# Attention steps of a graph layer without their loop, and half of the gathered rows added on TensorE

## The chip, the cores and the metric

The kernel runs on one core of a Trainium2 chip. The metric is the device time of one execution in microseconds, the median of several runs. The engines are TensorE (PE in the profile; PEld is its weight load), VectorE (DVE), ScalarE (ACT), GpSimd (POOL) and SyncE (SP, which only issues transfers here).

## The reference

One layer over 2500 nodes with 256 features and 80000 edges: a graph attention, a mixing product and a mixture of eight experts. The change touches the attention alone. What it computes, cut to the part that matters:

```python
xl = (x @ W_l).reshape(N, HEADS, HEAD_DIM)      # 4 heads of 64
xr = (x @ W_r).reshape(N, HEADS, HEAD_DIM)
e = xl[src] + xr[dst]
e = jnp.where(e >= 0, e, NEG_SLOPE * e)
score = jnp.einsum('ehd,hd->eh', e, att)
m = jax.ops.segment_max(score, dst, num_segments=N)
ex = jnp.exp(score - m[dst])
denom = jax.ops.segment_sum(ex, dst, num_segments=N)
alpha = ex / (denom[dst] + SM_EPS)
agg = jax.ops.segment_sum(alpha[:, :, None] * xl[src], dst, num_segments=N)
```

The edges are sorted by `dst`.

## The kernel before

The attention stage, `attend`, goes through the sorted edges in 176 steps, called quads, of four groups (G = 4) of 128 edges. Eight quads are a run (RUN), two runs a turn (RING = 16 quads), and there are 11 turns. `over_quads` writes out the first and the last turn and puts the nine between into a loop, so an engine holds 16 quads of code for them; addresses and semaphore thresholds in the loop come from registers. Every engine runs its own version of the same loop over quads, and semaphores tie them together. For quad q:

- SyncE loads `e_drow` (the target of each edge, spread over 128 partitions, L964) and `e_xr` (128 rows of xr, each split in three bf16 parts, L965) into four rotating buffers, and stores the running sums of the quad 16 steps back (L980).
- GpSimd gathers the four groups of xl rows, 128 x 260 fp32 each, with one indirect transfer per group (L1014). There are buffers for 16 quads, and the gather of quad q waits for the product of quad q - 16 (`prod`). The indices of a run of eight quads are first copied from `src_cols` to `e_idx` (L1007), twice per turn.
- VectorE makes the selection matrix `e_sel` two quads ahead (L1031). TensorE multiplies it with `e_xr` (`edges`, L1218: 4 groups x 3 parts, 12 bf16 products of 256 columns), which gives xr[dst] of every edge in two PSUM banks; banks alternate by quad.
- VectorE adds the gathered rows to these (`sum_edges`, L1040, two operations of 128 x 512), takes the positive part times the attention weights over all four groups (`relus`, L1048, 128 x 1024) and sums it by head (`scores`, L1055). The linear part of the leaky relu comes with the gathered row.
- Eleven quads later ScalarE takes the exponent (L1297) and multiplies the gathered rows with it, 16 copies of 128 x 64 (L1301, `e_prod`). Twelve quads later TensorE sums these by target with a selection matrix that VectorE makes (L1063): `sums`, L1262, four fp32 products of 260 columns, each of which the trace shows as two passes. VectorE adds the result to the running sums (`add_sums`, L1077).
- At the end of each run, in the first five quads of the next, the maxima of the run's scores are found: scans on VectorE, transposes on TensorE, a decay on ScalarE. I call these the closing steps. ScalarE's products of a run wait for its `e_diff` (L1147).

The order on an engine is that in which its `quad` function calls these parts. Engines execute in order, so an instruction that waits holds up all that stands behind it on its engine. Where the text below says step, a quad is meant.

## Time and profile before

| | us |
|---|---|
| median of three runs | 1959.8 (1956.9 to 1965.11) |
| profiled execution | 1963.8 |
| its span | 1962.1 |
| busy: TensorE, VectorE | 1224.7, 1141.8 |
| busy: ScalarE, GpSimd | 870.3, 796.9 |
| first gather starts | 229.1 |
| last gather starts | 1468.7 |

The span is what the engines' records cover; the profiled execution's own time has 1.7 us around it. The attention stage lies between about 229 and 1542 us. Busy times say what an engine executed, not what set the end; the timelines of several engines over the same few microseconds say who stood still while who worked. "Idle before" in brackets is the time an engine stood before a row, with what released it: an instruction of another engine, "issue" (nothing that the profile shows) or "remote" (a semaphore whose setter isn't seen).

### The profile page before, as it was taken

How to read it: one execution, taken by the hardware profiler on the slowest of the kernel's cores; microseconds unless marked ns; L12 is line 12 of the kernel's file. 1: busy time of each engine (PE TensorE's matmuls, PEld its weight loads, DVE VectorE, ACT ScalarE, POOL GpSimd, SP SyncE). 2: the span in 40 equal slices, each digit the busy share in tenths (PEclk: the TensorE clock that was granted, in tenths of full speed). 3: DMA queues.
4: the chain of work that ended last, by engine and by line, in shares of the span. 5: the costliest groups of instructions: out<-in, count | busy, mean ns of one | idle time of the engine just before them, and what ended most of it. 6: DMA issues, size and time to landing. Idle time of an engine off the chain costs nothing. (4 is left out here: it accounts for less than half of the span.)

```text
span 1962.1 us, 24702 instructions
## 1 busy us (share of the span) xinstructions
PE 1224.7 (62%) x5321; PEld 869.1 (44%) x5321; DVE 1141.8 (58%) x2208; ACT 870.3 (44%) x3346; POOL 796.9 (41%) x907
## 2 busy tenths in 40 slices
PE   2599513666666666566666765655657696499950
PEld 1476302444444444444544554444445465255530
DVE  3670215787777776787878776767766382000018
ACT  0241000556565655666665665656649422122211
POOL 3111372455555555555555555554540412200014
PEclk9998755788787887888898777877868865699985
DMA  4220243465555655565656555555540500144403
GB/s 155 78 93 13 70 117 90 122 155 140 146 135 154 158 145 142 142 159 138 165 149 163 147 155 141 146 144 135 152 119 31 154 1 21 49 119 119 118 27 95
DMA packets 161282, 230.60 MB, mean 118 GB/s; under 512 B 36421, under 2 KB 134078, under 8 KB 160766
## 3 DMA queue, kind: packets, MB, share of 16 engines
q1 hardware_dynamic: 121220, 124.33, 21.8%
q0 software_dynamic: 37056, 102.46, 21.0%
q10 hardware_dynamic: 2880, 2.66, 0.4%
q14 instruction: 110, 0.89, 0.2%
q8 instruction: 16, 0.26, 0.1%
HBM read 186.36 MB, written 42.99 MB: 117 GB/s over the span
## 5 line engine op out<-in xcount | busy, mean ns | idle before, releaser
L1014 POOL DMA_INDIRECT e_xl<-d_xl,e_idx x704 | 670.6, 953 | 544.0 <-ACT e_prod L1301 310.4
L1301 ACT ACTIVATE e_prod<-e_xl,e_prod 128x64 f32<-128x64 f32 x2816 | 692.3, 334 | 10.9 <-issue 5.0
L1262 PE MATMUL bank<-e_prod,e_selt 128*128 128x260 f32 x1408 | 460.9, 484 | 210.2 <-ACT e_prod L1301 133.7
L1262 PEld LDWEIGHTS bank<-e_prod,e_selt 128*128 128x128 f32 x1408 | 322.2, 240 | 303.2 <-issue 223.4
L1218 PE MATMUL bank<-e_xr,e_sel 128*128 128x256 bf16 x2112 | 327.1, 309 | 160.0 <-issue 112.9
L1218 PEld LDWEIGHTS bank<-e_xr,e_sel 128*128 128x128 bf16 x2112 | 232.2, 111 | 245.6 <-issue 172.0
L1040 DVE TENSOR_TENSOR e_edge<-bank,e_xl 128x512 f32<-128x512 f32 x352 | 224.9, 678 | 165.4 <-remote 118.9
L1048 DVE SCALAR_TENSOR_TENSOR e_edge<-e_edge,bank 128x1024 f32<-128x1024 f32 x176 | 212.6, 1208 | 0.1
L1055 DVE TENSOR_REDUCE e_score<-e_edge 128x16 f32<-128x1024 f32 x176 | 212.3, 1206 | 0.3
L1297 ACT ACTIVATE e_prod<-e_diff 128x16 f32<-128x16 f32 x176 | 39.1, 222 | 304.8 <-remote 196.6
L1077 DVE SCALAR_TENSOR_TENSOR e_acc<-e_acc,keep_cols,bank 128x260 f32<-128x260 f32 x154 | 72.9, 473 | 133.6 <-remote 77.9
L1710 DVE COPY f_y<-bank 98x256 f32<-98x256 f32 (+1 forms) x32 | 11.3, 417 | 227.3 <-PE bank L1681 227.3
L1063 DVE TENSOR_TENSOR e_selt<-bank,cyclic_cols 128x512 f32<-128x512 f32 x176 | 119.7, 680 | 0.0
L1290 ACT ACTIVATE e_rr<-e_drop 1x4 f32<-1x4 f32 x22 | 4.5, 205 | 251.0 <-DVE e_drop L1128 153.2
L1667 PE MATMUL bank<-f_rowst,w_rows 128*128 128x391 f32 x256 | 88.7, 505 | 5.5 <-ACT f_rowst L1691 4.9
L1743 POOL MEMSET c_subst<- 128x512 f32 x3 | 1.4, 523 | 220.2 <-POOLq L1626 220.2
L1673 PE MATMUL bank<-f_hid,w_rows 128*128 128x391 f32 x256 | 85.5, 491 | 0.0
L1031 DVE TENSOR_SCALAR e_sel<-e_drow,lane 128x512 bf16<-128x512 bf16 x176 | 63.1, 359 | 10.0 <-DMA e_xr<-d_xr 9.9
L1667 PEld LDWEIGHTS bank<-f_rowst,w_rows 128*128 128x128 f32 x256 | 49.0, 194 | 41.8 <-issue 9.3
L1673 PEld LDWEIGHTS bank<-f_hid,w_rows 128*128 128x128 f32 x256 | 48.4, 189 | 35.8
L1695 ACT ACTIVATE f_hid<-bank,b_cols 128x391 f32<-128x391 f32 x64 | 37.6, 588 | 57.1 <-PE bank L1667 57.1
L1246 PE MATMUL bank<-ident,e_tops 128*128 128x128 f32 x22 | 8.8, 402 | 74.0 <-DVE e_tops L1141 74.0
(310 smaller groups left out, 1131.4 us busy)
## 6 DMA issues: line engine op xcount, KB each, us to landing
e_xr<-d_xr SPq DMA_DIRECT2D x176, 192.0 KB
d_hist<-e_acc SPq DMA_DIRECT2D x176, 130.0 KB
e_drow<-d_rel SPq DMA_DIRECT2D x176, 128.0 KB
w_rows<-in_L_ffn_w_dram SPq DMA_DIRECT2D x16, 1024.0 KB
e_xl<-d_xl,e_idx POOLq DMA_INDIRECT x704
e_rows<-d_rows SPq DMA_DIRECT2D x22, 192.5 KB
d_xr<-a_xr SPq DMA_DIRECT2D x20, 192.0 KB
d_in<-zero SPq DMA_DIRECT2D x3, 1024.0 KB
```

The source lines that it names most:

```text
L1014: pool.indirect_dma_start(xl[:, q.slot * G + g, :], None, m.d_xl, bass.IndirectOffsetOnAxis(ap=idx[p][:, at:at + 1], axis=0)).then_inc(gat ...
L1031: dve.tensor_scalar(sel[:, b, :], drow[:, r, :], m.lane[:, 0:1], None, ALU.is_equal).then_inc(s["sel"], 1)
L1040: dve.tensor_tensor(edge[:, b, 2 * i:2 * i + 2, :], ps_edge[b][i][:, :].rearrange("p (g c) -> p g c", g=2), xl[:, q.slot * G + 2 * i:q.slo ...
L1048: dve.scalar_tensor_tensor(out=edge[:, b, :, :], in0=edge[:, b, :, :], scalar=0.0, in1=att_relu.unsqueeze(1).to_broadcast([P, G, DIM]), op ...
L1055: dve.tensor_reduce(score[:, p, :, q.at * G:q.at * G + G].rearrange("p h g -> p g h"), edge[:, b, :, :].rearrange("p g (h c) -> p g h c", ...
L1063: dve.tensor_tensor(selt[:, b, :, :], lane_up.unsqueeze(1).to_broadcast([P, G, P]), m.cyclic[:, bass.ds(q.k * G, G)].unsqueeze(2).to_broad ...
L1077: dve.scalar_tensor_tensor(out=flat(acc[:, r, :, :]), in0=flat(before), scalar=m.keep[:, bass.ds(q.k, 1)], in1=ps_agg[q.slot % 2], op0=ALU ...
L1218: last = pe.matmul(ps_edge[b][g // 2][:, g % 2 * DIM:g % 2 * DIM + DIM], sel[:, b, g * P:g * P + P], xr[:, r, part * DIM:part * DIM + DIM] ...
L1262: last = pe.matmul(ps_agg[b], selt[:, b, g, :], flat(prod[:, b, g, :, :]), start=(g == 0), stop=(g == G - 1))
L1301: last = act.activation(prod[:, b, g, h, 0:HEAD], xl[:, q.slot * G + g, h * HEAD:h * HEAD + HEAD], ACT.Copy, scale=prod[:, b, g, h, HEAD:H ...
L1667: last = pe.matmul(m.bank[2 + f % 2][:, 0:CAP], w1[:, q, half, f * P:f * P + P], rowst[:, half, :], start=(half == 0), stop=(half == 1))
L1673: last = pe.matmul(m.bank[4 + out][:, 0:CAP], w2[:, q, f, out * P:out * P + P], hid[:, f, :], start=(f == 0), stop=(f == FCH - 1))
```

## The change

- The loop is gone: all 176 quads are written out on each engine, with constant addresses and thresholds.
- GpSimd's copy of indices is gone. The gathers take their indices from `src_cols`.
- TensorE adds the gathered rows of groups 0 and 1 itself: after the three bf16 parts of a group follows one fp32 product of the gathered rows with an identity matrix into the same sums. It takes groups 2 and 3 first, then waits for the gathers of its quad, then groups 0 and 1. The identity (128 x 128) is the weight, the 256 columns of gathered rows move past it.
- VectorE adds only groups 2 and 3. The relu of groups 0 and 1 reads PSUM directly, with the attention weights from SBUF; groups 2 and 3 have a relu of their own.
- TensorE's products of quad q now wait for the relu of quad q - 2 on groups 0 and 1, which frees the bank, and for the sum on 2 and 3.

```diff
-def over_quads(eng, body, behind=0):
-    for slot in range(RING):
-        body(Quad(0, slot))
-    with eng.Fori(1, TURNS - 1) as turn:
-        for slot in range(RING):
-            body(Quad(turn, slot))
-    for slot in range(RING + behind):
-        body(Quad(TURNS - 1, slot))
+def over_quads(body, behind=0):
+    for k in range(QUADS + behind):
+        body(Quad(k // RING, k % RING))
...
             def quad(q):
-                p = q.slot // RUN
-                if q.at == 0:
-                    if q.since(2 * RUN):
-                        pool.wait_ge(s["summed"], 2 * q.k - 2 * RUN)
-                    pool.tensor_copy(idx[p][:, :], m.idx[:, bass.ds(q.run * SUBS_RUN, SUBS_RUN)]).then_inc(s["idx"], 1)
-                    pool.wait_ge(s["idx"], q.run + 1)
                 if q.since(RING):
                     pool.wait_ge(s["prod"], q.k - RING + 1)
                 settle(pool, m)
                 for g in range(G):
-                    at = q.at * G + g
+                    at = q.k * G + g
                     pool.indirect_dma_start(xl[:, q.slot * G + g, :], None, m.d_xl, bass.IndirectOffsetOnAxis(
-                        ap=idx[p][:, at:at + 1], axis=0)).then_inc(gathered[q.slot], 16)
+                        ap=m.idx[:, at:at + 1], axis=0)).then_inc(gathered[q.slot], 16)
...
-                for i in range(2):
-                    dve.tensor_tensor(edge[:, b, 2 * i:2 * i + 2, :],
-                                      ps_edge[b][i][:, :].rearrange("p (g c) -> p g c", g=2),
-                                      xl[:, q.slot * G + 2 * i:q.slot * G + 2 * i + 2, 0:DIM], ALU.add).then_inc(s["summed"], 1)
+                dve.tensor_tensor(edge[:, b, 2:4, :], ps_edge[b][1][:, :].rearrange("p (g c) -> p g c", g=2),
+                                  xl[:, q.slot * G + 2:q.slot * G + 4, 0:DIM], ALU.add).then_inc(s["summed"], 1)
...
-                dve.wait_ge(s["summed"], 2 * q.k + 2)
-                dve.scalar_tensor_tensor(out=edge[:, b, :, :], in0=edge[:, b, :, :], scalar=0.0,
-                                         in1=att_relu.unsqueeze(1).to_broadcast([P, G, DIM]),
+                dve.scalar_tensor_tensor(out=edge[:, b, 0:2, :], in0=ps_edge[b][0][:, :].rearrange("p (g c) -> p g c", g=2), scalar=0.0,
+                                         in1=m.att_relu[:, :].unsqueeze(1).to_broadcast([P, 2, DIM]),
+                                         op0=ALU.max, op1=ALU.mult).then_inc(s["relu"], 1)
+                dve.wait_ge(s["summed"], q.k + 1)
+                dve.scalar_tensor_tensor(out=edge[:, b, 2:4, :], in0=edge[:, b, 2:4, :], scalar=0.0,
+                                         in1=att_relu.unsqueeze(1).to_broadcast([P, 2, DIM]),
                                          op0=ALU.max, op1=ALU.mult).then_inc(s["relu"], 1)
...
                 if q.since(2):
-                    pe.wait_ge(s["summed"], 2 * q.k - 2)
-                for g in range(G):
+                    pe.wait_ge(s["summed"], q.k - 1)
+                    pe.wait_ge(s["relu"], 2 * q.k - 3)
+                for g in (2, 3, 0, 1):
+                    out = ps_edge[b][g // 2][:, g % 2 * DIM:g % 2 * DIM + DIM]
                     for part in range(3):
-                        last = pe.matmul(ps_edge[b][g // 2][:, g % 2 * DIM:g % 2 * DIM + DIM], sel[:, b, g * P:g * P + P],
-                                         xr[:, r, part * DIM:part * DIM + DIM], start=(part == 0), stop=(part == 2))
+                        last = pe.matmul(out, sel[:, b, g * P:g * P + P], xr[:, r, part * DIM:part * DIM + DIM],
+                                         start=(part == 0), stop=(part == 2 and g >= 2))
+                    if g < 2:
+                        if g == 0:
+                            pe.wait_ge(gathered[q.slot], (q.turn + 1) * 64)
+                        last = pe.matmul(out, m.ident[:, :], xl[:, q.slot * G + g, 0:DIM], start=False, stop=True)
                 last.then_inc(s["edges"], 1)
```

What this makes of the order on three engines. First VectorE, one plain quad inside the loop before; ISA and REGISTER_ALU are register work:

```order
L1040 TENSOR_TENSOR e_edge<-bank,e_xl 128x512 x2
L1031 TENSOR_SCALAR e_sel<-e_drow,lane 128x512
L1047 ISA
L1048 SCALAR_TENSOR_TENSOR e_edge<-e_edge,bank 128x1024
L1077 REGISTER_ALU
L1077 SCALAR_TENSOR_TENSOR e_acc<-e_acc,keep_cols,bank 128x260
L1063 ISA
L1063 TENSOR_TENSOR e_selt<-bank,cyclic_cols 128x512
L1055 TENSOR_REDUCE e_score<-e_edge 128x4x4
```

and the same quad after (line numbers are those of the changed kernel):

```order
L1026 TENSOR_TENSOR e_edge<-bank,e_xl 128x512
L1018 TENSOR_SCALAR e_sel<-e_drow,lane 128x512
L1032 SCALAR_TENSOR_TENSOR e_edge<-bank,att_relu 128x512
L1036 SCALAR_TENSOR_TENSOR e_edge<-e_edge,bank 128x512
L1065 SCALAR_TENSOR_TENSOR e_acc<-e_acc,keep_cols,bank 128x260
L1051 TENSOR_TENSOR e_selt<-bank,cyclic_cols 128x512
L1043 TENSOR_REDUCE e_score<-e_edge 128x4x4
```

One of two sums has gone, the relu is in two halves of which the first no longer follows a sum, and the register work is gone. Then TensorE, the products of two quads with the sums between them, inside the loop before:

```order
L1213 REGISTER_ALU
L1215 ISA
L1218 MATMUL bank<-e_xr,e_sel 128x256 x12
L1257 REGISTER_ALU
L1262 MATMUL bank<-e_prod,e_selt 128x260 x4
L1213 REGISTER_ALU
L1215 ISA
L1218 MATMUL bank<-e_xr,e_sel 128x256 x12
```

and after:

```order
L1208 MATMUL bank<-e_xr,e_sel 128x256 x9
L1213 MATMUL bank<-e_xl,ident 128x256
L1208 MATMUL bank<-e_xr,e_sel 128x256 x3
L1213 MATMUL bank<-e_xl,ident 128x256
L1256 MATMUL bank<-e_prod,e_selt 128x260 x4
```

Two fp32 products stand in the quad's products, the first behind nine bf16 ones, and the sums come after them. Last GpSimd, the start of a run inside the loop before:

```order
L1007 ISA
L1007 COPY e_idx<-src_cols 128x32
L1008 REGISTER_ALU
L1010 REGISTER_ALU
L1014 DMA e_xl<-d_xl,e_idx 128x260 x4
```

and the whole stage after, from its last memset on:

```order
L993 MEMSET e_acc 128x1040
L1001 DMA e_xl<-d_xl,src_cols 128x260 x704
L947 UNCONDITIONAL_BRANCH
```

Nothing but waits stands between the gathers any more.

## Rows read from the trace of the kernel before

**Rows 1.** The page's busy table: us, share of the span, instructions.

```profile
PE 1224.7 (62%) x5321; PEld 869.1 (44%) x5321; DVE 1141.8 (58%) x2208; ACT 870.3 (44%) x3346; POOL 796.9 (41%) x907
```

**Rows 2.** The page's groups: count | busy, mean ns | idle before.

```profile
L1014 POOL DMA_INDIRECT e_xl<-d_xl,e_idx x704 | 670.6, 953 | 544.0 <-ACT e_prod L1301 310.4
...
L1218 PE MATMUL bank<-e_xr,e_sel 128*128 128x256 bf16 x2112 | 327.1, 309 | 160.0 <-issue 112.9
...
L1040 DVE TENSOR_TENSOR e_edge<-bank,e_xl 128x512 f32<-128x512 f32 x352 | 224.9, 678 | 165.4 <-remote 118.9
L1048 DVE SCALAR_TENSOR_TENSOR e_edge<-e_edge,bank 128x1024 f32<-128x1024 f32 x176 | 212.6, 1208 | 0.1
```

**Rows 3.** Stretches of line L1055 alone, both halves of one turn: start:end, length.

```profile
837.50:891.20 53.70, 9.63 (x8) 0.85 0.59 153
891.20:945.40 54.20, 9.65 (x8) 0.81 0.58 148
```

**Rows 4.** One turn: PE, PEld, DVE, ACT, POOL busy, PEclk, DMA share, GB/s.

```profile
504.00:617.00 113.00, 73.30 (x336) 52.99 (x336) 84.72 (x148) 66.80 (x278) 59.87 (x65) 0.77 0.54 141
```

**Rows 5.** Waits between 504 and 1391 us: total, times, longest.

```profile
POOL e_xl L1014 <- ACT e_prod L1301: 228.2, 58, 7.7
...
DVE e_acc L1077 <- remote: 84.7, 16, 8.2
...
DVE e_edge L1040 <- remote: 68.6, 30, 6.4
```

**Rows 6.** VectorE's timeline, 641 to 656 us: start, us, operation [idle before].

```profile
641.18 1.28 DVE L1040 TENSOR_TENSOR e_edge<-bank,e_xl 128x512 f32<-128x512 f32 x2
642.38 0.56 DVE L1031 TENSOR_SCALAR e_sel<-e_drow,lane 128x512 bf16<-128x512 bf16 x1
642.86 1.20 DVE L1048 SCALAR_TENSOR_TENSOR e_edge<-e_edge,bank 128x1024 f32<-128x1024 f32 x1
643.98 0.47 DVE L1077 SCALAR_TENSOR_TENSOR e_acc<-e_acc,keep_cols,bank 128x260 f32<-128x260 f32 x1
...
652.62 1.29 DVE L1040 TENSOR_TENSOR e_edge<-bank,e_xl 128x512 f32<-128x512 f32 x2 [6.43 <-remote]
```

**Rows 7.** GpSimd's timeline around 520 us and around 650 us.

```profile
520.87 0.22 POOL L1007 COPY e_idx<-src_cols 128x32 int32 x1
521.98 0.97 POOL L1014 DMA_INDIRECT e_xl<-d_xl,e_idx  x1 [0.89 <-POOL e_idx L1007]
...
648.14 0.95 POOL L1014 DMA_INDIRECT e_xl<-d_xl,e_idx  x1 [0.30 <-issue]
649.39 0.95 POOL L1014 DMA_INDIRECT e_xl<-d_xl,e_idx  x1 [0.30 <-issue]
```

**Rows 8.** ScalarE's timeline from 536 us and from 646 us on.

```profile
536.02 3.93 ACT L1301 ACTIVATE e_prod<-e_xl,e_prod 128x64 f32<-128x64 f32 x16
...
646.88 0.35 ACT L1301 ACTIVATE e_prod<-e_xl,e_prod 128x64 f32<-128x64 f32 x1 [0.37 <-issue]
648.27 0.35 ACT L1301 ACTIVATE e_prod<-e_xl,e_prod 128x64 f32<-128x64 f32 x1 [1.04 <-issue]
```

**Rows 9.** TensorE's timeline from 536 us on, at half, then at full clock.

```profile
536.01 3.81 PE L1262 MATMUL bank<-e_prod,e_selt 128*128 128x260 f32 x8 [4.01 <-ACT e_prod L1301]
539.61 2.44 PE L1218 MATMUL bank<-e_xr,e_sel 128*128 128x256 bf16 x12
541.89 1.92 PE L1262 MATMUL bank<-e_prod,e_selt 128*128 128x260 f32 x8
543.64 1.47 PE L1218 MATMUL bank<-e_xr,e_sel 128*128 128x256 bf16 x12
```

**Rows 10.** The first gathers: VectorE's longest idle, and GpSimd after its copy.

```profile
276.33 1.29 DVE L1040 TENSOR_TENSOR e_edge<-bank,e_xl 128x512 f32<-128x512 f32 x2 [26.00 <-remote]
...
270.18 0.97 POOL L1014 DMA_INDIRECT e_xl<-d_xl,e_idx  x1 [0.81 <-POOL e_idx L1007]
```

More of the change, by code:

```diff
@@ L887, in exists @@
         return not self.known() or 0 <= self.k < QUADS
-def over_quads(eng, body, behind=0):
-    for slot in range(RING):
-        body(Quad(0, slot))
-    with eng.Fori(1, TURNS - 1) as turn:
-        for slot in range(RING):
-            body(Quad(turn, slot))
-    for slot in range(RING + behind):
-        body(Quad(TURNS - 1, slot))
+def over_quads(body, behind=0):
+    for k in range(QUADS + behind):
+        body(Quad(k // RING, k % RING))
 def attend(nc, ctx, m, a):
     sb = lambda name, shape, dt=F32: ctx.enter_context(nc.sbuf_tensor(name, shape, dt))
-    s = sem_set(nc, m.sems, "att", "init idx sel edges summed relu score lin turned run top ends heads fwd bwd carried drop cols raised tops topped diff rr f fac ex prod selt agg old acc rows* links fixed")
+    s = sem_set(nc, m.sems, "att", "init sel edges summed relu score lin turned run top ends heads fwd bwd carried drop cols raised tops topped diff rr f fac ex prod selt agg old acc rows* links fixed")
     loaded = [m.sems.enter_context(nc.semaphore(f"att_loaded{r}")) for r in range(4)]
@@ L908, in attend @@
     gathered = [m.sems.enter_context(nc.semaphore(f"att_gathered{r}")) for r in range(RING)]
-    idx = [sb(f"e_idx{q}", [P, SUBS_RUN], I32) for q in range(2)]
     xl = sb("e_xl", [P, RING * G, ROW])
@@ L989, in _ @@
             sp.wait_ge(s["init"], 1)
-            over_quads(sp, quad, behind=STORE_LAG)
+            over_quads(quad, behind=STORE_LAG)
             for r in range(4):
@@ L1012, in quad @@
                 for g in range(G):
-                    at = q.at * G + g
+                    at = q.k * G + g
                     pool.indirect_dma_start(xl[:, q.slot * G + g, :], None, m.d_xl, bass.IndirectOffsetOnAxis(
-                        ap=idx[p][:, at:at + 1], axis=0)).then_inc(gathered[q.slot], 16)
-            over_quads(pool, quad)
+                        ap=m.idx[:, at:at + 1], axis=0)).then_inc(gathered[q.slot], 16)
+            over_quads(quad)
         @block.vector
@@ L1053, in scores @@
                 b, p = q.slot % 2, q.slot // RUN
-                dve.wait_ge(s["relu"], q.k + 1)
+                dve.wait_ge(s["relu"], 2 * q.k + 2)
                 dve.tensor_reduce(score[:, p, :, q.at * G:q.at * G + G].rearrange("p h g -> p g h"),
@@ L1205, in _ @@
                 select(Quad(0, k))
-            over_quads(dve, quad, behind=CLOSE_LAG)
+            over_quads(quad, behind=CLOSE_LAG)
         @block.tensor
@@ L1281, in quad @@
                     carry_cols(o)
-            over_quads(pe, quad, behind=CLOSE_LAG)
+            over_quads(quad, behind=CLOSE_LAG)
         @block.scalar
@@ L1322, in _ @@
             act.wait_ge(s["init"], 4)
-            over_quads(act, quad, behind=WEIGH_LAG)
+            over_quads(quad, behind=WEIGH_LAG)
 def node_update(nc, ctx, m, a):
```

## The prediction

> **What bounds the kernel now.** I read the busy table first. No engine is full: TensorE has 62% of the span, VectorE 58% [rows 1]. The costly groups all lie in the attention stage, and the longest in wall time is GpSimd's: 704 gathers of 953 ns, four to a step of 128 x 4 edges [rows 2]. On GpSimd's timeline inside a burst one gather follows the other every 1.25 us (0.95 busy, 0.30 issue), so the four of a step take 5.0 us [rows 7]. The stage's 176 steps therefore cannot take less than 176 x 5.0 = 880 us.
>
> The table by stretches says how long a step does take: 54 us for 8 steps in either half of a 16-step turn, 6.75 each [rows 3], and 113 us for 16 steps in another turn [rows 4], 7.1 each. I use 6.9. VectorE alone would do it in 4.7: on its timeline two sums take 1.20 from start to start of the next operation, and the whole step runs without a gap [rows 6]. Gathers alone would do it in 5.0. What is added is the interplay of the two, and the timelines of one stretch on four engines show it.
>
> Between 645 and 652.6 us GpSimd issues gathers without a break [rows 7], VectorE stands still for 6.43 us, released by "remote" [rows 6], and ScalarE, whose sixteen copies depend on nothing but each other, executes single ones 0.35 us long with 0.37 or 1.04 us between their end and the next start instead of back to back [rows 8]. So this is no missing operand: while a burst of gathers lasts, the other engines crawl. I call it a hold. It ends when GpSimd has run out of gathers it may issue, here 2.3 us after the last one (650.34 to 652.62). The first steps show it naked: GpSimd issues 64 gathers in a row there, and VectorE has one idle of 26.00 us [rows 10]. In the stretch 504 to 1391 the holds cost VectorE 84.7 + 68.6 = 153 us, and GpSimd in turn waits 228.2 us for ScalarE's products (which free the buffers of the step 16 back) [rows 5]. The kernel swings between the two: burst, hold, buffers run out, the others work, the next burst. That swing sets the end; the busy times matter only by what they do to it.
>
> **The change part by part.** The sum is made against the profiled execution, 1963.8 us (span 1962.1); the median of the three runs is 4.0 lower.
>
> *Index copies.* Once per run of 8 steps GpSimd copied 32 columns of indices: 0.22 for the copy and 0.89 until the next gather, against 0.30 between others [rows 7], so 0.81 too much. 22 times: 17.8 us. GpSimd is always inside a burst there, so I take it whole: -18. Bounds 0 and -24 (22 x 1.11).
>
> *VectorE.* Per step two sums and one 1024-wide product go; one sum and two 512-wide products come. From start to start: before 1.20 + 1.12 = 2.32 (641.18 to 642.38, and 642.86 to 643.98) [rows 6]; a 512-wide operation takes 0.60 of that, so three take 1.80. A 512-wide relu that reads PSUM isn't in the trace; it is nearest to the sum, which also reads PSUM (678 ns) [rows 2]. Saved 0.52 per step, 92 us of work over 176. Where does it reach the end? Not in a hold, and not where GpSimd is late anyway. It does in the three closing steps of each of 22 runs, where GpSimd waits for ScalarE, ScalarE for VectorE: 66 x 0.52 = 34, of which I take half, 17, because some of these steps lie beside bursts. And in some 17 steps at the start (after the first 64 gathers) and after the last gather: 9. Together -26; bounds 0 and -92.
>
> *TensorE.* Two fp32 products per step come, each two passes, 704 passes in all. A pass of 260 columns is 1.92 / 8 = 0.24 us long at full clock and 3.81 / 8 = 0.48 at half [rows 9]; both clocks occur all the time, since the granted clock is 0.77 of full over a turn [rows 4], near the middle of 1.2 and 2.4 GHz. So a step gets 0.96 or 1.9 us more on TensorE, 169 to 335 us in all. Cover: TensorE is idle for about 40 of 113 us in a turn [rows 4], and the projection products of a step are ready before VectorE asks for them. The cover fails in one place: after a long hold TensorE starts at half clock, does sums (3.81), then the products of the next step (2.44) [rows 9], and these are used at once. There the added 1.9 minus the about 1.0 that VectorE also comes earlier (two steps of 0.52) is exposed: 0.9, at the 16 long waits of "DVE e_acc <- remote" [rows 5]: +14. Bounds 0 and +335. TensorE now also waits for the gathers of its step, with the sums of the step 12 back queued behind; a gather is issued when the product of the step 16 back is done and products lag 11 steps, so about 5 steps ahead, 5 x 6.9 = 34 us, and I cost this at nothing. If that lead were gone, each step would wait for a gather, up to 5 us.
>
> *The loop.* Register arithmetic for addresses and thresholds goes from every engine: by the order of instructions some 17 per step, against 8 more for TensorE and 1 or 2 for VectorE. On a free engine these are hidden behind data work (VectorE's step has no gap [rows 6]). In a hold every instruction is slow, so fewer of them ought to help: about 7 fewer of about 108 per step. 7% of the 153 us of holds [rows 5], carried from 128 to 144 steps: -12. Bounds 0 and -170 (all holds gone). The loop's backward branch costs nothing that I can see: the half turn that holds it takes 54.2 us, the other 53.7 [rows 3].
>
> The Trainium skill (Runtime: NRT & Kernel Launch, "Instruction fetch mechanics") says that a taken branch to a target outside two pages of instructions stalls until a DMA has fetched it, and that written-out code avoids this. By that rule the unrolling would be the larger part of the gain; rows 3 show no such cost, and the sum above leaves it out.
>
> Sum: 1963.8 - 18 - 26 + 14 - 12 = 1921.8; less the 4.0 between profiled run and median: 1918.
>
> **The rivals.** *TensorE becomes the bound (slower), 0.27.* The granted clock of 0.77 means that nearly half the time is at half clock. If that share of the 144 middle steps, 144 x 0.46 = 66, pays 1.9 and saves only 0.52, it is 66 x 1.38 = +91; with the copies' -18 and the 4.0 it is 2033. If half of it is covered, 1987. It decides from the point at which TensorE ends a step's products later than VectorE ends the relu of the step before. For it: TensorE at half clock needs 3.81 + 2.44 + 1.9 = 8.2 us for a step, more than the 6.9 of today. Against it: at full clock 1.92 + 1.47 + 0.96 = 4.4 [rows 9], and TensorE works off its queue during holds.
>
> *Nothing moves, 0.14.* If a cycle is only gathers (5.0 per step) and ScalarE's first product after a hold, neither VectorE's nor TensorE's work counts, and some of the copies' time is given back: 1963.8 - 9 - 4 = 1951 to 1965. For it: ScalarE needs 3.93 us for the sixteen copies of a step whatever VectorE does [rows 8], and GpSimd's waits are waits for ScalarE [rows 5].
>
> *The back edge does cost, 0.10.* A hold lies at the end of each turn. If its 4.5 us were the branch (10 turns), 45 us would go beside the rest: 1918 - 45 = 1873. Against it: an equal hold stands in mid turn and the halves are equal [rows 3].
>
> *Longer holds, 0.07.* The 26.00 us hold ended at 276.33, 6 us after GpSimd's copy had left its gap at 270.18 [rows 10]. If these gaps let the others through and are gone, each of 22 runs may lose some 3 us: +66 - 40 = 1990.
>
> The forecast keeps 0.42.
>
> **How the numbers follow.** A measurement of this kernel can tell about 0.5%, 10 us, from no change, so "faster" is under 1950 and "slower" over 1970. Faster: 0.42 + 0.10 and a little of the second rival, 0.55. Same: 0.14. Slower: 0.31. The forecast's own range, with VectorE's and the holds' terms at a third or double, is 1885 to 1950. The stated range reaches to the branch rival and to the half-covered TensorE rival: 1862 to 2000. The likeliest time is 1918.
>
> **What would show it.** In the changed profile GpSimd must show 704 gathers at the same 1.25 us with no copy between. VectorE's step should be near 4.2 where nothing holds it. If the forecast is right, the steps per turn of 16 (where the loop had its turns) take 102 to 108 us, and the "remote" waits of VectorE stay, a little shorter. If TensorE has become the bound, VectorE's sum waits for TensorE's new fp32 line rather than for "remote", and the time is over 1980. If the holds are gone or halved, instruction count or branch was their cause and my time is far too high. The prediction fails, too, if the added instructions of TensorE count as much for the holds as the removed register work.

## The result: slower by 1.4%, or faster by 4%, by whether the chip held its engines

In the comparison for which the forecast was made the kernel before took 1961.0 us (median) and the changed kernel 1982.7: ratio 1.0143, interval 1.0072 to 1.0213. Forecast were 1918 and "faster". The time is inside the stated range (1862 to 2000), outside the forecast's own (1885 to 1950), and the direction is wrong. Ratios and their 95% intervals compare fast runs only, while the times beside them are medians of all runs, so a few pairs of times don't divide to their ratio.

One fact has to come first. The changed kernel was compared three times, each time beside the kernel before on one chip, and came out on both sides:

| comparison | before, us | changed, us | ratio (interval) | holds in the traces |
|---|---|---|---|---|
| first | 1961.0 | 1982.7 | 1.014 (1.007 to 1.021) | yes |
| `after_again` | 1659.3 | 1597.0 | 0.960 (0.954 to 0.966) | none in steady work |
| `after_third` | 1937.7 | 1992.0 | 1.029 (1.020 to 1.039) | yes |

The holds, on which the whole prediction was built, are not a property of the kernel alone. Of seven comparisons five had them and two did not. The kernel before tells the two apart by its time, 1938 to 1961 us or 1659 to 1663, and within a comparison all kernels are alike, save those to which a long pause was added. The results number the chips, and two numbers (4 and 7) occur once in either condition.

**The profile after (first comparison).** The page's busy table, against [rows 1]:

```profile
PE 1336.2 (68%) x6025; PEld 946.2 (48%) x6025; DVE 1047.5 (53%) x2208; ACT 869.9 (44%) x3346; POOL 789.4 (40%) x885
```

VectorE has 94 us less work, TensorE 112 us more. The page's groups (count | busy, mean ns | idle before), against [rows 2]:

```profile
L1001 POOL DMA_INDIRECT e_xl<-d_xl,src_cols x704 | 668.7, 950 | 599.3 <-ACT e_prod L1295 368.2
...
L1213 PE MATMUL bank<-e_xl,ident 128*128 128x256 f32 x704 | 243.9, 432 | 12.4 <-issue 6.8
L1026 DVE TENSOR_TENSOR e_edge<-bank,e_xl 128x512 f32<-128x512 f32 x176 | 119.6, 680 | 244.1 <-remote 197.8
...
L1032 DVE SCALAR_TENSOR_TENSOR e_edge<-bank,att_relu 128x512 f32<-128x512 f32 x176 | 119.2, 677 | 0.0
L1036 DVE SCALAR_TENSOR_TENSOR e_edge<-e_edge,bank 128x512 f32<-128x512 f32 x176 | 118.3, 672 | 0.0
```

Each operation costs what it was expected to: the relu that reads PSUM 677 ns, as the sum. But the idle before VectorE's sum rose from 165.4 to 244.1 us, and GpSimd's idle from 544.0 to 599.3. The stretch of [rows 5], in the columns of [rows 4]; in each pair the first line is of the scores' line alone (L1043, L1055), so its count is the number of steps. After:

```profile
504.00:1391.00 887.00, 149.33 (x124) 0.84 0.56 143
...
504.00:1391.00 887.00, 634.55 (x3109) 461.51 (x3110) 588.56 (x1140) 518.16 (x2155) 471.00 (x496) 0.84 0.56 143
```

Before:

```profile
504.00:1391.00 887.00, 154.29 (x128) 0.81 0.57 148
...
504.00:1391.00 887.00, 562.43 (x2688) 413.54 (x2688) 674.76 (x1169) 532.59 (x2213) 490.93 (x528) 0.81 0.57 148
```

VectorE's work per step went from 674.76 / 128 = 5.27 to 588.56 / 124 = 4.75, that is 0.52 less, as the prediction said. The step went from 887 / 128 = 6.93 to 887 / 124 = 7.15. The waits of the same stretch say what took its place, against [rows 5]:

```profile
POOL e_xl L1001 <- ACT e_prod L1295: 251.3, 57, 12.4
...
DVE e_edge L1026 <- remote: 111.6, 27, 11.2
...
DVE e_acc L1065 <- remote: 96.2, 17, 9.2
...
DVE e_run L1081 <- DMA x_rows<-in_x_dram: 42.5, 7, 9.2
```

VectorE's two "remote" waits were 153 us and are 208, and a third line (L1081, put down to a DMA that was issued in the first 10 us of the kernel and can't be what it waits for) stands in holds for another 42.5. In the kernel before that line (L1093) had 6.1. One of these holds, on GpSimd's, then VectorE's timeline (start, us, operation [idle before]); eleven more gathers follow the first without a wait:

```profile
486.05 0.94 POOL L1001 DMA_INDIRECT e_xl<-d_xl,src_cols  x1 [7.94 <-ACT e_prod L1295]
...
499.80 0.95 POOL L1001 DMA_INDIRECT e_xl<-d_xl,src_cols  x1 [0.30 <-issue]
508.28 0.94 POOL L1001 DMA_INDIRECT e_xl<-d_xl,src_cols  x1 [7.53 <-ACT e_prod L1295]
...
494.72 0.68 DVE L1036 SCALAR_TENSOR_TENSOR e_edge<-e_edge,bank 128x512 f32<-128x512 f32 x1
503.40 0.42 DVE L1081 TENSOR_TENSOR_SCAN e_run<-e_rows,bank 128x128 f32<-128x128 f32 x1 [8.01 <-DMA x_rows<-in_x_dram]
```

If a pause of over 1.5 us ends a burst, bursts of twelve gathers or more were 18 of 70 between 400 and 1350 us in the trace before, and are 28 of 64 now. In the rows above a burst runs, VectorE is held for 8 us, GpSimd then waits 7.5 us for ScalarE, and the next burst starts.

The first steps have the longest holds. GpSimd issues its first 64 gathers from 230.56 us on without a gap, and VectorE stands twice:

```profile
262.98 0.69 DVE L1026 TENSOR_TENSOR e_edge<-bank,e_xl 128x512 f32<-128x512 f32 x1 [16.28 <-remote]
...
307.78 0.69 DVE L1026 TENSOR_TENSOR e_edge<-bank,e_xl 128x512 f32<-128x512 f32 x1 [41.40 <-remote]
```

So a hold can end for one step in the middle of a burst, at 262.98 here, with no copy near it.

TensorE's new line shows 1.06 us for the two passes of a product at half clock and 0.60 at full. From its start to the start of the next product it is 0.85 and 0.44, where the prediction had 0.96 and 0.48:

```profile
505.57 2.12 PE L1208 MATMUL bank<-e_xr,e_sel 128*128 128x256 bf16 x9
507.49 1.06 PE L1213 MATMUL bank<-e_xl,ident 128*128 128x256 f32 x2
508.34 0.84 PE L1208 MATMUL bank<-e_xr,e_sel 128*128 128x256 bf16 x3
...
512.74 0.60 PE L1213 MATMUL bank<-e_xl,ident 128*128 128x256 f32 x2
513.18 0.49 PE L1208 MATMUL bank<-e_xr,e_sel 128*128 128x256 bf16 x3
```

### The profile page after: what moved, and what is told of

Same layout as the page of the kernel before. It is cut to its first block and busy times, and to the rows that moved or that the text cites. A ratio compares the mean times of both kernels' runs of the same rounds, so it can differ in the third digit from the quotient of the medians.

```text
span 1978.6 us, 23673 instructions
## 1 busy us (share of the span) xinstructions
PE 1336.2 (68%) x6025; PEld 946.2 (48%) x6025; DVE 1047.5 (53%) x2208; ACT 869.9 (44%) x3346; POOL 789.4 (40%) x885
## 5 line engine op out<-in xcount | busy, mean ns | idle before, releaser
L1001 POOL DMA_INDIRECT e_xl<-d_xl,src_cols x704 | 668.7, 950 | 599.3 <-ACT e_prod L1295 368.2
L1256 PE MATMUL bank<-e_prod,e_selt 128*128 128x260 f32 x1408 | 405.0, 431 | 125.2 <-ACT e_prod L1295 48.8
L1208 PE MATMUL bank<-e_xr,e_sel 128*128 128x256 bf16 x2112 | 351.0, 305 | 171.1 <-issue 86.8
L1256 PEld LDWEIGHTS bank<-e_prod,e_selt 128*128 128x128 f32 x1408 | 285.7, 212 | 215.6 <-issue 153.9
L1208 PEld LDWEIGHTS bank<-e_xr,e_sel 128*128 128x128 bf16 x2112 | 225.7, 108 | 286.7 <-issue 204.5
L1213 PE MATMUL bank<-e_xl,ident 128*128 128x256 f32 x704 | 243.9, 432 | 12.4 <-issue 6.8
L1026 DVE TENSOR_TENSOR e_edge<-bank,e_xl 128x512 f32<-128x512 f32 x176 | 119.6, 680 | 244.1 <-remote 197.8
L1043 DVE TENSOR_REDUCE e_score<-e_edge 128x16 f32<-128x1024 f32 x176 | 212.1, 1205 | 0.3
L1213 PEld LDWEIGHTS bank<-e_xl,ident 128*128 128x128 f32 x704 | 126.1, 223 | 22.1 <-issue 7.7
L1032 DVE SCALAR_TENSOR_TENSOR e_edge<-bank,att_relu 128x512 f32<-128x512 f32 x176 | 119.2, 677 | 0.0
L1036 DVE SCALAR_TENSOR_TENSOR e_edge<-e_edge,bank 128x512 f32<-128x512 f32 x176 | 118.3, 672 | 0.0
```

What stands on the lines that cost most here:

```text
L1001: pool.indirect_dma_start(xl[:, q.slot * G + g, :], None, m.d_xl, bass.IndirectOffsetOnAxis(ap=m.idx[:, at:at + 1], axis=0)).then_inc(gath ...
L1026: dve.tensor_tensor(edge[:, b, 2:4, :], ps_edge[b][1][:, :].rearrange("p (g c) -> p g c", g=2), xl[:, q.slot * G + 2:q.slot * G + 4, 0:DIM ...
L1032: dve.scalar_tensor_tensor(out=edge[:, b, 0:2, :], in0=ps_edge[b][0][:, :].rearrange("p (g c) -> p g c", g=2), scalar=0.0, in1=m.att_relu[ ...
L1036: dve.scalar_tensor_tensor(out=edge[:, b, 2:4, :], in0=edge[:, b, 2:4, :], scalar=0.0, in1=att_relu.unsqueeze(1).to_broadcast([P, 2, DIM]) ...
L1043: dve.tensor_reduce(score[:, p, :, q.at * G:q.at * G + G].rearrange("p h g -> p g h"), edge[:, b, :, :].rearrange("p g (h c) -> p g h c", ...
L1208: last = pe.matmul(out, sel[:, b, g * P:g * P + P], xr[:, r, part * DIM:part * DIM + DIM], start=(part == 0), stop=(part == 2 and g >= 2))
```

## The experiments

**Theories.** H: where holds occur, they give back what is saved. P: TensorE's added passes are the cost. U: the written-out code, or the missing index copies, are. C (added after the first four experiments): the sign hangs on whether holds occur.

### Both halves of the change alone

`e_unroll_only` has the changed kernel's loops and the additions of before:

```
-                dve.tensor_tensor(edge[:, b, 2:4, :], ps_edge[b][1][:, :]...
+                for i in range(2):
+                    dve.tensor_tensor(edge[:, b, 2 * i:2 * i + 2, :], ...
```

> The 176 steps written out and the index copies gone, but all four groups added on VectorE as before: half of the change. Theory H (holds give back what is saved: every engine but GpSimd crawls while gathers run without a break, and anything that lets GpSimd issue longer bursts lengthens them): the loss comes from denser bursts, some of it from the copies' gaps gone; 1950 to 1975 us. Theory P (the loss is TensorE's added fp32 passes): without them the prediction's own terms for copies and instructions hold, 1961 - 18 - 12 = 1931. Theory U (written-out code is itself the loss): as slow as the changed kernel, 1983 or more.

`e_pe_add_only` has the loop and the index copies, with the changed kernel's sum_edges, relus and edges:

> The loop and the index copies stay; groups 0 and 1 are added in PSUM by the fp32 identity product: the other half of the change. Theory H: VectorE's saved 0.52 us a step is given back by longer holds, and TensorE's new work is not itself late; 1955 to 1980. Theory P: the fp32 passes cost 14 to 91 us in the prediction's working and VectorE's saving gives 26 at most; 1980 to 2000, with VectorE waiting for TensorE's fp32 line. Theory U: 1961 - 26 + 14 = 1949 or less.

`e_no_add` is the changed kernel less its identity products, so it leaves out the gathered rows of groups 0 and 1:

```
-                    if g < 2:
-                        if g == 0:
-                            pe.wait_ge(gathered[q.slot], (q.turn + 1) * 64)
-                        last = pe.matmul(out, m.ident[:, :], xl[:, q.slot * G + g, 0:DIM], start=False, stop=True)
```

> The changed kernel without the two identity products of a step: groups 0 and 1 are left without their gathered rows (that addition is left out), so VectorE has its saving of 0.52 us a step and TensorE no more work than before. Theory H: still no gain to speak of, 1950 to 1980, with holds as long as in the changed kernel. Theory P: the prediction's sum without TensorE's term, 1918 - 14 = 1904, up to 1930. Theory U: between, 1983 - 14 = 1969.

`e_copies` is the changed kernel with this back in front of each 8 steps' gathers:

```
+                    pool.tensor_copy(idx[p][:, :], m.idx[:, bass.ds(q.run * SUBS_RUN, SUBS_RUN)]).then_inc(s["idx"], 1)
+                    pool.wait_ge(s["idx"], q.run + 1)
```

> The changed kernel with GpSimd's index copy of 32 columns put back once per 8 steps. Theory H, gap form (the copies' gaps shortened holds): faster than the changed kernel by 5 to 20 us, 1963 to 1978. Theory H, plain form (a gap of 0.8 us once in 32 gathers is too rare to matter): 1980 to 1990. The prediction's term for the copies: 18 us slower than the changed kernel, 2001.

Measured, in one comparison in which the kernel before took 1663.4 us: 1623.7 (ratio 0.975, 0.971 to 0.980), 1611.9 (0.969, 0.963 to 0.974), 1584.6 (0.954, 0.950 to 0.959) and 1617.0 (0.972, 0.968 to 0.976). No theory had such times, since there were no holds: no engine has a wait for "remote", and GpSimd issued its 704 gathers with no gap over 0.9 us in three of the four (1.8 in e_unroll_only). They are the change's parts without holds, to be read with the next comparison. Of the four only two were repeated where holds occur; the copies put back and the loop with the identity products were not, so there the copies and the loop are not told apart.

### The two kernels themselves, without holds

`after_again` and `before_again` are unchanged.

> The changed kernel itself. In the four runs before this, GpSimd issued its 704 gathers without a single wait and no engine was held; the kernel before took 1663 us there and 1961 where the first comparison was made. Theory C (the sign hangs on the chip: where holds occur they give everything back, where they don't the gathers' 5.1 us per step or VectorE's step is the bound): without holds the changed kernel takes 1605 to 1620 against 1663, ratio 0.965 to 0.975; with holds 1.01 to 1.02 at 1960 to 2000. Theory P (TensorE's work costs 14 to 91 us everywhere): ratio over 1.0 in either case.

> The kernel before, for its profile on the chip of this comparison. Theory C: without holds VectorE is busy over 95% of the attention stage, since its step of about 5.3 us (closing work in it) is longer than the four gathers of 5.0, and GpSimd issues without waits; 1663 us. With holds: as in the first profile, VectorE 76% busy, 1961 us.

Measured: 1597.0 against 1659.3, and 1666.7 for the profiled kernel before. Theory C has the sign, though the ratio of 0.960 lies a little under its 0.965 to 0.975; theory P falls in its strict form. What bounds each is plain in these traces. Before, 400 to 1000 us, the scores' line alone and then all engines (VectorE is the third pair); the groups of the page's kind below:

```profile
400.00:1000.00 600.00, 130.39 (x109) 0.87 0.72 187
...
400.00:1000.00 600.00, 432.18 (x2264) 326.33 (x2262) 569.20 (x997) 449.23 (x1882) 423.13 (x457) 0.87 0.72 187
...
L1040 DVE TENSOR_TENSOR e_edge<-bank,e_xl 128x512 f32<-128x512 f32 x352 | 224.1, 675 | 11.2 <-DMA e_xl<-d_xl,e_idx 9.1 <-issue 1.9
```

600 / 109 = 5.5 us a step (5.3 expected), VectorE busy 95%, and 11.2 us of idle before its sum where [rows 2] have 165.4. The changed kernel:

```profile
400.00:1000.00 600.00, 142.49 (x119) 0.97 0.78 203
...
L1001 POOL DMA_INDIRECT e_xl<-d_xl,src_cols x704 | 671.3, 954 | 214.4 <-issue 200.7 <-ACT e_prod L1295 13.7
```

600 / 119 = 5.04 us, four gathers at 1.25; of 214.4 us between gathers 200.7 are issue. It is bound by GpSimd's gathers.

In this condition the parts can be priced. VectorE's saving, within one comparison: 1623.7 - 1584.6 = 39 us; the prediction had 26. The index copies: e_copies less the changed kernel is 0.972 - 0.960 = 0.012 of 1660, 19 us; the prediction had 18. TensorE's products: 0.960 - 0.954 = 0.006, 10 us; it had 14. The last two are differences between two comparisons and are known to 12 us either way, so TensorE's is not clear of zero. And the loop's back edge, which it had at nothing: ScalarE's timeline of before_again where a turn begins,

```profile
399.75 0.30 ACT L1310 COPY e_fwd_link<-links 1x128 bf16 x1 [2.07 <-issue]
...
403.18 0.23 ACT L1297 ACTIVATE e_prod<-e_diff 128x16 f32<-128x16 f32 x1 [2.94 <-issue]
```

5.0 us in which ScalarE waits for nothing that the profile shows. The same pair stands at the start of each of the eight turns behind a branch, 4.4 to 6.7 us together, and in e_unroll_only nowhere. VectorE pays 3.45 us a step later, behind TensorE's transposes. VectorE's line L1103, the copy that waits there, in before_again, and the same line (L1090) in e_unroll_only:

```profile
  PE bank L1235: 29.7, 9
...
  PE bank L1222: 0.5, 1
```

29 us go with the loop. The first step of a turn took 9.0 to 10.4 us in before_again in each of the eight turns behind a branch, and 6.3 where none lay before it and in every turn of e_unroll_only. The Trainium skill's rule (Runtime: NRT & Kernel Launch, "Instruction fetch mechanics": a taken branch out of the fetched pages stalls for its target) agrees with this, 1.7 to 3.9 us at a time on ScalarE; the trace shows the idle time, not the fetch. In [rows 3] it didn't show beside the holds.

### The same parts where holds occur

> The changed kernel without the identity products (groups 0 and 1 are left without their gathered rows, as in the earlier run of it), on another chip. Where holds occur, theory H expects no gain over the kernel before, 1950 to 1980 us, since VectorE's saving alone lengthens the bursts; theory P (TensorE's work is what costs there) expects 1880 to 1930. Where none occur it repeats 0.954 of the kernel before within 0.005, 10 us under the changed kernel.

> The steps written out and the index copies gone, all additions on VectorE as before, once more. Where holds occur, the changed kernel without its identity products came out at 0.998 of the kernel before. Theory H (any work saved comes back as holds) expects about the same here, 0.99 to 1.01. If written-out code alone lengthens the bursts and VectorE's saving does help, this is slower than that, 1.01 to 1.03; if VectorE's saving is what feeds the bursts, faster, 0.97 to 0.985. Without holds it repeats 0.975.

Measured: the changed kernel without its identity products 1953.9 us against 1955.5 (0.998, 0.993 to 1.003); the written-out kernel with all additions on VectorE 1954.4 against 1943.8 (1.005, 1.001 to 1.009). With the changed kernel's 1.014 and 1.029 beside them: writing out, worth 40 us without holds, is worth nothing; VectorE's 0.5 us a step is worth 0.7% (14 us, between 1 and 26); TensorE's products cost 1.7 to 3.2%, 32 to 61 us, not 10. These are differences between comparisons too, known to 12 to 21 us, but both of TensorE's are clear of zero. The next experiment, which does have the products, lies 32 us over e_no_add_2 in the same comparison. The trace of e_no_add_2 shows how the saving goes (scores' line; all engines; waits of 504 to 1391 us):

```profile
504.00:1391.00 887.00, 153.42 (x127) 0.81 0.56 147
...
504.00:1391.00 887.00, 556.50 (x2670) 407.83 (x2668) 600.93 (x1155) 530.99 (x2209) 484.77 (x511) 0.81 0.56 147
...
DVE e_acc L1065 <- remote: 123.4, 20, 8.6
DVE e_run L1081 <- DMA x_rows<-in_x_dram: 51.2, 8, 8.0
DVE e_edge L1026 <- remote: 41.2, 22, 7.0
```

VectorE works 600.93 / 127 = 4.73 a step instead of 5.27, and the step is still 6.98. Its three kinds of hold are 216 us, and the same three lines of the kernel before 84.7 + 68.6 + 6.1 = 159. Whatever the line and the releaser, VectorE's idle times of over 2 us in this stretch are 232 us (42 of them) instead of 164 (30): 68 us more, and 127 x 0.54 = 69 us was saved. So VectorE's saving comes back as holds, as theory H has it. For TensorE's part theory P has the size right, but not the way: VectorE hardly waits for TensorE's new line, 23.7 us before its sum in the changed kernel against 24.8 for the projection products in this one. The cost, too, appears as "remote".

### GpSimd's lead

> The changed kernel, but GpSimd may gather a step's rows only when the product of the step 14 back is done, not 16 back: it can be 3 steps ahead of VectorE instead of 5. Where holds occur, theory H (a hold lasts until GpSimd has used up the gathers it may issue) expects each hold 5 to 8 us shorter, and 1850 to 1960 us against the changed kernel's 1983; a hold that ends by itself after a time would stay, and the shorter lead then costs: 1990 to 2050. Where none occur (1597 before) GpSimd is the bound and has had no credit to spare: 1597 to 1615, with waits of GpSimd for ScalarE's products of a few us.

```
-                    pool.wait_ge(s["prod"], q.k - RING + 1)
+                    pool.wait_ge(s["prod"], q.k - 13)
```

Measured: 1985.7 against 1955.5 (1.018, 1.008 to 1.028), as the changed kernel. The expectation was wrong on both counts: the time lies in neither range. Bursts of twelve are 27, as 28 in the changed kernel, and VectorE's two "remote" waits 205 us, as 208. So what ends a burst is not the lead alone. My reading, not shown by a run, is that ScalarE's products made while the burst runs feed it, and two steps less of lead shift VectorE against GpSimd and leave the cycle as it is.

### A pause between the gathers

The changed kernel with a memset behind the gathers of a step; only its width, or how often it comes, differs:

```
+                if q.k:
+                    pool.wait_ge(s["pause"], q.k)
+                pool.memset(pause[:, :], 0.0).then_inc(s["pause"], 1)
```

> The changed kernel with a memset of 128x1280 on GpSimd behind the four gathers of every step, about 1.2 us each with nothing else added: a step's gathers take 6.3 us instead of 5.1. Where holds occur, theory H (a hold needs a long unbroken burst) expects most of them gone and 1800 to 1930 us; if a hold needs only the number of gathers, not their density, the time stays at 1980 or rises to 2100. Where none occur, theory C (gathers alone are the bound of the changed kernel there) expects 176 x 1.2 = 211 us more than the changed kernel, about 1820; if VectorE or TensorE were the bound, less than half of it.

> The changed kernel with the memset of 128x1280 on GpSimd behind the four gathers of each step, once more, in the hope of a chip on which holds occur. There, theory H in its density form (a hold needs about 6 us of gathers without a break, and 1 us of pause every 5 us lets the other engines through) expects holds rarer and 1780 to 1930 us; if a hold follows from a number of gathers and not from their density, 1985 to 2100. Without holds it repeats 1.064 of the kernel before, 6.06 us a step.

> The changed kernel with a memset of 128x16 on GpSimd behind the four gathers of each step: hardly any time, about 0.1 us, but an instruction of another kind between them. Where holds occur: if it is the other instruction that lets the engines through, holds go and it takes 1600 to 1640 us; if it is the idle microsecond of the gather queue, they stay and it takes 1960 to 2000. Without holds: 1597 to 1620.

> The same with 128x512, which adds some 0.4 us to a step's 5.0: 5.4 us. Density theory: somewhere between no pause (holds in most steps) and 1 us (none) is the point; here, if below it, 1640 to 1680 us with and without holds; if above it, holds remain, 1850 to 1980 where they occur, and 1640 to 1680 elsewhere.

> The memset of 128x1280, but only behind every second step: 1.06 us after 8 gathers in a row, 10.0 us, so on average the same pause as the half one. Where holds occur, they begin 5 to 7 us after a burst does, so the theory of the unbroken burst expects them to stay (1850 to 1980), and the theory of the mean rate expects the same time as the half pause. Without holds: 1670 to 1700.

> The changed kernel with a memset of 128x1024 on GpSimd behind the four gathers of each step, about 0.8 us net: 5.8 us a step. A pause of 0.37 us left all holds, 1.06 us left none. If the point lies under 0.8, 1720 to 1750 us with and without holds elsewhere, and that is then the fastest version that no session slows; if it lies over it, 1850 to 1970 where holds occur.

| kernel | memset | added per step, us | us | kernel before, us | ratio (interval) |
|---|---|---|---|---|---|
| e_pause_min | 128x16 | 0.0 | 2004.9 | 1953.0 | 1.031 (1.022 to 1.041) |
| e_pause_half | 128x512 | 0.4 | 1966.3 | 1953.0 | 1.009 (1.004 to 1.013) |
| e_pause_second | 128x1280, every second step | 0.5 | 1968.8 | 1953.0 | 1.012 (1.003 to 1.021) |
| e_pause_1024 | 128x1024 | 0.8 | 1835.0 | 1937.7 | 0.945 (0.937 to 0.953) |
| e_pause_2 | 128x1280 | 1.04 | 1774.2 | 1943.8 | 0.910 (0.903 to 0.916) |
| e_pause, no holds | 128x1280 | 1.04 | 1767.1 | 1659.3 | 1.064 (1.059 to 1.069) |

One microsecond of extra work per step on the engine that feeds all others takes the changed kernel from 1.014 and 1.029 to 0.910 where holds occur, and its time is then the same within 0.4% in either condition. Where none occur it costs 6.4% against the kernel before and 170 us against the changed kernel (expected were 211; 176 x 1.04 would be 183), so it is no version that beats both kernels everywhere. GpSimd's timeline of e_pause_2:

```profile
701.27 0.95 POOL L1002 DMA_INDIRECT e_xl<-d_xl,src_cols  x1 [0.31 <-issue]
702.22 1.18 POOL L1006 MEMSET e_pause<- 128x1280 f32 x1
703.56 0.95 POOL L1002 DMA_INDIRECT e_xl<-d_xl,src_cols  x1 [0.17 <-issue]
```

From start to start 2.29 instead of 1.25, so 1.04 added. Its steps and engines in 504 to 1200 us, and VectorE's wait that was 111.6 us in the changed kernel (both 504 to 1391):

```profile
504.00:1200.00 696.00, 139.03 (x115) 0.93 0.64 168
...
504.00:1200.00 696.00, 539.20 (x2858) 413.55 (x2857) 588.90 (x1042) 479.51 (x1994) 572.27 (x573) 0.93 0.64 168
...
DVE e_edge L1030 <- remote: 11.2, 8, 2.5
```

696 / 115 = 6.05 us a step, all of it GpSimd's 5.0 + 1.04; VectorE's longest idle in this stretch is 4.4 us (11.2 in the changed kernel), and the clock granted is 0.93. With 0.4 us instead (e_pause_half) they stand as before:

```profile
504.00:1200.00 696.00, 118.14 (x98) 0.84 0.53 143
...
DVE e_acc L1069 <- remote: 78.2, 15, 7.8
DVE e_edge L1030 <- remote: 66.3, 26, 13.3
```

So it isn't an instruction of another kind that lets the engines through: the smallest pause is as slow as none. With 5 us of gathers between pauses, 0.8 us ends more than half of the holds' cost and 1.04 all of it; the point lies between 0.4 and 1.04. Whether it is the unbroken burst or the mean rate of the gathers that counts stays open. e_pause_second came out as both theories expected: it has the long pause behind 8 gathers, but its mean, 0.5 us a step, is also that of the half pause, and over all five kernels the gain follows the mean (none up to 0.5, some at 0.8, all at 1.04). A run with 2 us behind every eighth gather would tell them apart. Of the expectations, e_pause_2 (1774) came out just under the range in which most holds go (1780 to 1930), e_pause_half on the side where holds remain; e_pause_1024 at 1835 lies between its two ranges, and e_pause_min 5 us over its own.

One thing about these runs the expectations left out: the memset also slows VectorE. Its `e_sel`, 354 ns in the changed kernel, takes 543 with the memset of 1024 columns, 760 in e_pause_2 and 945 in e_pause. So the pause is not purely one between gathers, and a pause without a memset was not tried.

### The kernel before with a pause

> The kernel before (loop, index copies, all additions on VectorE) with the memset of 128x512 behind the four gathers of each step. Theory C (the change's own gain is there once no engine is held): its VectorE needs about 5.2 us a step, so it takes 1690 to 1740 us where the changed kernel with the same pause takes 40 to 60 less. If holds remain it shows as little difference from the kernel before as they leave.

> The kernel before with the memset of 128x1280 behind each step's gathers. Theory H: its holds go as well, GpSimd's 6.06 us a step bound it like the changed kernel, plus 22 index copies: 1775 to 1810 us in any session. If holds in the loop version have another cause, it stays at 1900 to 1960 where they occur.

Measured: with 128x512 a median of 1964.8 against 1953.0 (0.997, 0.990 to 1.003), no better and no worse, so holds remain; with 128x1280 1797.6 against 1937.7 (0.926, 0.917 to 0.935), as theory H expected. The holds of the kernel before go in the same way, so the change is not their cause. With the same long pause the changed kernel is 0.910 and this one 0.926. The difference of 1.6% (1.1 either way, since it is between two comparisons) is near what the copies and the loop's edge cost without holds; VectorE's part would then be hidden behind the gathers, which no run shows by itself.

### The third run of the changed kernel

> The changed kernel once more. Where holds occur it repeats 1.010 to 1.020 of the kernel before (the parts there: written out alone 1.005, with VectorE's saving but no identity products 0.998, so TensorE's products cost 1.2 to 2.2%); where none occur, 0.955 to 0.965.

Measured: 1992.0 against 1937.7 (1.029, 1.020 to 1.039), more than the 1.010 to 1.020 expected. Slower where holds occur is no accident of one comparison; its size is 1 to 4%.

## Why the prediction was wrong

It named the right mechanism and then treated it as a fixed cost. "The busy times matter only by what they do to it" stands in its first part; in the sum, savings are counted as if the holds stayed what they were. That is the step that failed. Where holds occur, VectorE's saving (-26 forecast) came back as holds, nothing of the copies and the loop's instructions (-18 and -12) reached the end, and what was added on TensorE cost 32 to 61 us instead of 14. That the stated range held the time is no merit of the sum: it reached that far for the TensorE rival.

- **VectorE, -26.** The size per step was right (0.52). What failed is that half of the 66 closing steps, and 17 others, let it reach the end. Where holds occur nearly all of it comes back: 69 us saved and 68 us more of idle in e_no_add_2, 14 us left in the time. Without holds it is worth 39.
- **Fewer instructions in holds, -12.** Wrong in sign for the whole: the written-out kernel has them gone and is at 1.005. Its three kinds of hold take 94.7 + 56.9 + 37.6 = 189 us in 504 to 1391 where the kernel before had 159.
- **Index copies, -18.** 19 us without holds; with holds nothing of it is to be found in e_unroll_2, which has neither copies nor loop. "GpSimd is always inside a burst there" misses that GpSimd waits for ScalarE after the burst (251.3 us in 504 to 1391), where a gain inside the burst can be lost again. That was the mechanism of the rival "nothing moves", which had 0.14. The copies alone were not tried there.
- **TensorE, +14.** 10 us without holds (not clear of zero), 32 to 61 with. The exposed place was guessed (sixteen long holds at 0.9). The bounds 0 to 335 held it, and the wait for the step's gathers, costed at nothing, cost nothing that the waits show. The rival "TensorE becomes the bound" has the sign and, at 1987, nearly the time, but not the evidence it asked for: VectorE waits 17.5 us for TensorE's fp32 line in 504 to 1391, against 208 for "remote".
- **The back edge, 0.** Wrong: 29 us where nothing covers it, found in rows of a trace without holds. The argument from [rows 3], that both half turns take the same, was no evidence, for each half held stands of its own: VectorE's were 7.5 and 2.9 us in one, 5.9 and 3.8 in the other. Eight branches are taken, not ten, at 3.6 us each on the first step of a turn.
- **"Longer holds", 0.07.** This rival had what happened: 1990 forecast for it, 1983 and 1992 measured. The number is luck, since its +66 was a guess and its reason isn't borne out: it took the end of the 26.00 us hold for the work of a copy's gap, but in the changed kernel a hold ended in mid burst at 262.98 with no copy near. Those ends, before and after, also contradict the reading that a hold lasts until GpSimd has run out of gathers. Gaps do matter, but 1.04 us behind eight gathers did nothing and behind four ended the holds, so one of 0.8 us in 32 should be too rare; that was not tried by itself.

Sum where holds occur: -18 - 26 + 14 - 12 = -42 forecast, +22 and +54 measured. Without holds -62 was measured (0.960, where the sum would give 0.979). The sum lacks the 29 us of the back edge and 13 of VectorE's saving; it has 12 too much for holds that weren't there, and copies and back edge together gave 40 us, not 19 + 29.

**What stays open.** Why some comparisons have holds and others none: durations of gathers (950 and 954 ns) and of VectorE's sums (680 and 677) are equal in both, and the kernels are the same. What the other engines lack in a hold: the traces show single instructions 0.35 us long and far apart, not what they wait for; that their instructions come late because the gathers hold up their supply was not tested. In five of six holds taken from the first two traces VectorE went on 2.3 to 2.7 us after the end of the last gather's instruction, 0.9 to 1.2 us after its last packets had moved, so the gathers' transfers may matter more than their issue. And why TensorE's products cost more there than without holds, though VectorE doesn't wait for them.

Of what the prediction said the profile would show: the gathers (950 ns, 0.30 between) and VectorE's unheld step of 4.2 us came so; the turns took 109 to 121 us, not 102 to 108; the "remote" waits did not get shorter.

## What to carry to other kernels

Where the profile ascribes waits to "remote" on several engines at once, find what switches them on before anything else is costed, with an experiment that changes the trigger (here 1 us of pause between gathers, worth 9%) and not the work around it. Work taken off an engine that waits like that came back as waiting here. If a kernel swings between two such conditions, its time without them should be known before a change is judged: this change is worth 4% on one side and -1 to -3% on the other, and its version with the long pause takes 1767 and 1774 us.

## What the runs showed of the hardware

- VectorE, ScalarE, TensorE and SyncE can be held while GpSimd issues gathers every 1.25 us. VectorE's longer holds are 4 to 13 us in steady work and up to 41 us in the first 64 gathers. Gathers of 5 us followed by 1.04 us of memset don't do it, with 0.4 us they do. The condition was there in five comparisons of seven.
- Without it, 704 gathers with no gap over 0.3 us (after_again) leave no engine with a wait for "remote".
- The granted clock was 0.84 in the changed kernel's 504 to 1391 us with holds, where TensorE was busy for 634.55 of 887 us (72%), and 0.97 in 400 to 1000 us without, where it was busy for 528.44 of 600 (88%).
- A loop's backward branch costs ScalarE 4.4 to 6.7 us per turn, 3.6 of which reach the end.
- A memset of 128x1280 on GpSimd beside VectorE's `e_sel` (128x512 bf16) takes it from 354 to 760 and 945 ns on average.
